# Scan of a state-space block: B put on the identity's diagonal and multiplied into du's transpose, in place of scaled copies of du

## The reference

```python
delta = softplus(dtp @ dt_w + dt_b)
A = -exp(A_log)
dA = exp(delta[..., None] * A)
dBu = (delta * xc)[..., None] * Bm[:, :, None, :]
def step(h, inp):
    dA_t, dBu_t, C_t = inp
    h = dA_t * h + dBu_t
    return (h, einsum('bds,bs->bd', h, C_t))
y = ys + xc * Dp
```

## Time and profile before

| | us |
|---|---|
| three runs | 457.71, 460.2, 460.31 |
| median | 460.2 |
| the profiled execution | 459.13 |
| its span, first to last instruction | 457.3 |
| PE / PEld busy | 404.7 / 265.1 |
| DVE / ACT / POOL busy | 284.4 / 234.2 / 138.6 |

### The profile page before, as it was taken

One profiled execution on the slowest core, in us unless ns is written; L12 is line 12 of the kernel. 1 busy time (PEld: TensorE's weight loads), 2 busy tenths in 40 slices (PEclk: granted clock), 3 DMA queues, 4 the chain that ended last, 5 costly groups with the idle time before them and its releaser, 6 DMA issues.

```text
span 457.3 us, 9931 instructions
## 1 busy us (share of the span) xinstructions
PE 404.7 (88%) x3990; PEld 265.1 (58%) x3990; DVE 284.4 (62%) x697; ACT 234.2 (51%) x433; POOL 138.6 (30%) x118
## 2 busy tenths in 40 slices
PE   3788998999989978997689999989999799999992
PEld 2445675546765836662466666754677456666662
DVE  5785985754757554326499888763466554444546
ACT  1225654737567055766699999314455552222220
POOL 5829643300013124130098989310001100000001
PEclk9899999999999988998899999999999999999997
DMA  7320000000000000003013332052000000000001
GB/s 184 78 72 1 3 4 2 1 3 1 4 4 0 1 0 2 1 0 93 16 69 97 112 97 76 1 187 90 3 3 4 2 0 1 0 0 2 0 1 46
DMA packets 17023, 14.42 MB, mean 32 GB/s; under 512 B 6435, under 2 KB 14147, under 8 KB 16979
## 3 DMA queue, kind: packets, MB, share of 16 engines
q1 hardware_dynamic: 15680, 13.09, 9.7%
q10 hardware_dynamic: 1299, 0.71, 0.5%
HBM read 13.22 MB, written 0.57 MB: 30 GB/s over the span
## 4 chain that ended last, share of the span: by engine, by line
PE 69%; DVE 13%; ACT 11%; issue 3%; DMA 1%; POOL 1%; ACTq 0%; POOLq 0%; DVEq 0%
PE PS L1695 7%; PE PS L1756 6%; PE PS L1760 6%; PE PS L1369 6%; PE PS L1787 6%; PE PS L1315 4%; PE PS L1301 4%; PE PS L1348 4%; ACT att L633 3%; PE PS L1682 3%; PE PS L1384 3%; PE PS L1611 2%; ACT att L795 2%; PE PS L1431 2%; PE PS L1310 2%
## 5 line engine op out<-in xcount | busy, mean ns | idle before, releaser
L633 ACT ACTIVATE att<-PS 77x512 f32<-77x512 f32 (+1 forms) x96 | 51.7, 591 | 45.7 <-PE PS L1372 45.7
L904 DVE TENSOR_REDUCE mxp<-PS 128x4 f32<-128x308 f32 (+1 forms) x96 | 48.0, 537 | 31.8 <-PE PS L1348 31.8
L496 POOL TENSOR_TENSOR rstd<-ve,neg_half 128x1 f32<-128x1 f32 x24 | 13.3, 556 | 120.1 <-DVE ve L966 120.1
L830 ACT ACTIVATE kM<-PS 128x512 f32<-128x512 f32 x32 | 19.1, 597 | 56.3 <-PE PS L1756 56.3
L1198 DVE TENSOR_TENSOR_SCAN big<-big,PS 128x768 f32<-128x768 f32 x22 | 38.2, 1746 | 7.2 <-PE PS L1682 7.2
L1254 DVE TENSOR_TENSOR big<-kM,PS 128x512 f32<-128x512 f32 x32 | 21.9, 688 | 27.3 <-PE PS L1760 26.0
L490 POOL TENSOR_TENSOR rstd<-ve,neg_half 128x4 f32<-128x4 f32 x6 | 6.2, 1032 | 103.7 <-DVE ve L860 103.7
L1301 PE MATMUL PS<-negsel,identb 128*128 128x512 bf16 x140 | 33.9, 386 | 2.2 <-DVE big L1006 1.7
L1756 PE MATMUL PS<-xT,V 128*128 128x512 f32 x64 | 32.9, 596 | 0.8 <-DVE xT L1242 0.8
L1760 PE MATMUL PS<-xT,V 128*128 128x512 f32 x64 | 32.7, 592 | 0.0
L1787 PEld LDWEIGHTS PS<-big 128*128 128x128 f32 x256 | 29.7, 192 | 3.3 <-issue 3.3
(11 more groups left out here) (349 smaller groups left out, 896.7 us busy)
## 6 DMA issues: line engine op xcount, KB each, us to landing
kM<-Cdram SPq DMA_DIRECT2D x6, 384.0 KB, 3.5
XH<-Cdram SPq DMA_DIRECT2D x5, 384.0 KB, 3.4
xT<-Cdram SPq DMA_DIRECT2D x5, 384.0 KB, 3.4
V<-in_L_ffn_Wg SPq DMA_DIRECT2D x1, 1024.0 KB, 5.4
V<-in_L_ffn_Wu SPq DMA_DIRECT2D x1, 1024.0 KB, 8.0
convw<-in_L_attn_conv_w SPq DMA_DIRECT2D x1, 512.0 KB
out_x<-X SPq DMA_DIRECT2D x2, 256.0 KB, 2.3
ctxN<-in_ctx ACTq DMA_DIRECT2D x1, 308.0 KB
```

The costliest lines, as they stand in the source:

```text
L633: A_(PT[0:nk, i % 2, g], bank4(at.bank("exp", i, g), nk), ACT.Exp, scale=at.scale)\
L904: V_.tensor_reduce(mxp[:, b % 3, g, 0:J], PS[:, at.bank("max", b, g), 0:J * nk].rearrange("p (j k) -> p j k", j=J), axis=AX.X, op=ALU.max) ...
```

## The change

`scale(s)` no longer scales duT. It multiplies the 128x128 identity by B for the tokens of piece k, which gives a diagonal matrix diagB, 128 x 128 for each of six pieces. `inputs(n)` multiplies: stationary operand duT (tokens x channels of half h), moving operand diagB; the result is du's piece with channels on partitions and each token's column scaled by its B. The call is a plain matmul instead of a transpose. The waits for duT go from `scale(0)`, and scale(0) and scale(1) stand ahead of decay(0). diagB has two sets of six in `att` and `qT`.

```diff
-    scaled = [[att[:, 1536 + 256 * k:1536 + 256 * (k + 1)] for k in range(NK)],
-              [qTflat[:, 256 * k:256 * (k + 1)] for k in range(4)] + [att[:, 3072 + 256 * k:3072 + 256 * (k + 1)] for k in range(2)]]
+    diagB = [att[:, 1536:1536 + W768].rearrange("p (k t) -> p k t", k=NK), qTflat[:, 0:W768].rearrange("p (k t) -> p k t", k=NK)]
...
         def scale(s):
             if s == 0:
                 dring.wait_copied(act, "BT")
-                act.wait_ge(event("duT0_copied"), 1)
-                act.wait_ge(event("duT1_copied"), 1)
             if s >= 2:
                 act.wait_ge(event("dBu_ready"), NH * (s - 1))
             for k in range(NK):
-                ins = A_(scaled[s % 2][k], duT[:, k, :], ACT.Identity, scale=BT[:, k, s:s + 1])
+                ins = A_(diagB[s % 2][:, k, :], ident[:], ACT.Identity, scale=BT[:, k, s:s + 1])
             ins.then_inc(event("scaled"), 1)

+        scale(0)
+        scale(1)
         decay(0)
         act.wait_ge(event("duT_ready"), 1)
         A_(duT[:, :, 0:128], PSflat[:, 4 * 512:4 * 512 + W768].rearrange("p (k d) -> p k d", k=NK), ACT.Identity)\
             .then_inc(event("duT0_copied"), 1)
         decay(1)
-        scale(0)
         decay(2)
-        scale(1)
...
             for k in range(NK):
-                ins = nc.tensor.transpose(dBu[n % NDB][:, 128 * k:128 * (k + 1)],
-                                          scaled[s % 2][k][:, 128 * h:128 * (h + 1)], ident[:])
+                ins = M_(dBu[n % NDB][:, 128 * k:128 * (k + 1)], duT[:, k, 128 * h:128 * (h + 1)], diagB[s % 2][:, k, :],
+                         start=True, stop=True)
             ins.then_inc(event("dBu_ready"), 1)
```

## The result

| | before | after |
|---|---|---|
| runs, us | 457.71 to 460.31 (6 runs) | 475.04 to 478.18 (6 runs) |
| median, us | 459.94 | 476.98 |
| profiled execution, us | 459.13 | 476.93 |
| its span, us | 457.3 | 475.1 |

The ratio is 1.0387, with a 95% interval of 1.0362 to 1.0412: 17.0 us slower by the medians, 17.8 by the ratio and by the two profiled executions. Forecast were 477.7 as a median (+17.5) and 476.6 for the profiled execution.

The account below looks back on a forecast made before the run. TensorE (PE) was taken to bound most of the scan, ScalarE its first quarter. Steps of 2.63 us gave +17.95, less 0.47 for the earlier start: +17.5 on 460.2, so 477.7 us, range 473.5 to 481.5.

Parts of the forecast that it names:

- The price of a call: TensorE's inputs: a float32 matmul is two records, 0.223 us against a transpose's 0.109; a step's inputs go from 0.66 to 1.34 us.
- rival 4: TensorE's inputs: a transpose is worth a factor of 4, 0.436 us a call; +57.4 us, 517.6; chance 1%.
- Rival 3: TensorE's inputs: weight loads of 0.19 us aren't hidden, 27 us on top, about 505; chance 2%.
- The start: Start of the scan: inputs(0) comes right after y_start, so the first scan and inputs(3) are 0.47 us earlier.
- The end of the stretch: From inputs(3) to the end of inputs(31), PE without a gap: 74.98 us instead of 57.03, ending near 305.7.
- ScalarE: Scaled copies of 128 instead of 256 elements: 1.70 us a step instead of 2.02, 10.3 us less busy, off the path.
- The bound of the kernel before: In the scan, ScalarE bounds the first quarter, PE the greater part from 247.5 us on, by the chain of waits.
- The bubbles: Gaps in PE's transpose groups during the scan, 1.77 us in all, put down to ScalarE's lateness; they go with the change.
- rival 2: TensorE's inputs: the added matmul costs what the transpose did, only the gains count; -2.9 us, 457.3; chance 4%.
- The moved calls: scale(0), scale(1) ahead of decay(0), no longer waiting for duT: decay(0) some 0.7 us later, duT's copy not moved.

Follow-up runs that it names:

- Experiment 1: Kernel before, scaled copies kept, but turned by a float32 matmul with the identity instead of a transpose: 478.97 us, ratio 1.0417.
- experiment 5: Changed kernel with duT and diagB in bf16, so a call is one record: 453.54 us, ratio 0.9889 to the kernel before.
- Experiment 3: Changed kernel with each diagonal written twice (256 columns), putting back ScalarE's old cost: 477.18 us, ratio 1.0372 to the kernel before.
- Experiment 4: Kernel before with scaled copies cut to 128 columns, second half's steps reading the first half's: 458.01 us, ratio 0.9971.
- experiment 6: Kernel before with h*C in bf16, the y accumulation two records in place of four: 457.48 us, ratio 0.9971.
- experiment 2: Changed kernel with scale(0) and scale(1) back behind decay(1) and decay(2): 476.54 us, ratio 1.0375 to the kernel before.
- experiment 8: Kernel before with diagonals and matmuls for s = 0 and 1 only, scaled copies and transposes after: 458.68 us, ratio 1.0004.
- 9: Changed kernel with duT, diagB and h*C all in bf16: 450.99 us, ratio 0.9841 to the kernel before.

## Why the prediction was right, and where it wasn't

- **The price of a call** (0.223 us from L1787's row, 1.34 a step): 1.34 in the chain at every step, 384 records. Experiment 1 shows that the kind of call alone does it, experiment 5 that the loss turns into a gain once the same call is one short record. The factor of 4 of rival 4 is refuted for this shape: 1.34 against 0.66 is 2.0. Rival 3 (weight loads that nothing hides) falls with the same 1.34.
- **The start**: inputs(0) was forecast for 225.63, the first scan for 227.18, inputs(3) for 230.72; the profile has 225.66, 227.19 and 230.74 (chain).
- **The end of the stretch**: forecast 230.72 + 74.98 = 305.70; the last accumulations begin at 305.79 (below, PE's records in order of time), 17.57 us after the 288.22 of the earlier trace rows.

```profile
304.45 1.50 PE L1679 MATMUL PS<-qT,big 128*128 128x128 f32 x12
305.79 2.75 PE L1692 MATMUL PS<-big,ident 128*128 128x512 f32 x8
```

- **ScalarE**: 128x128 copies of 386 ns (forecast near 385), 32% idle from 247 to 305 us (forecast 35% of the scan), 8.0 us less of busy time (forecast 10.3, a term that stood outside the sum); DVE's wait for PE up to 0.9 us a step, as forecast. Experiment 3 shows that the relief is worth nothing there.
- **The bound of the kernel before** was named too simply. The prediction read from the chain that PE was the bound from 247.5 us on, although it had ScalarE at 2.02 us a step and PE at 1.95. The chain's own starts settle it:

```profile
257.48 0.72 PE PS L1682 x6
...
285.64 0.79 PE PS L1682 x6
```

  That is 14 steps in 28.16 us, 2.01 a step: ScalarE's pace and not PE's. Experiment 4 relieved ScalarE and the step became 1.96; experiment 6 relieved PE and it stayed at 2.02. The chain hid this: PE's weight loads waited for ScalarE only 0.3 us at a time, and such a wait stands in the chain as a longer group of PE. For the sum nothing hung on it, since the change adds 0.68 us a step to PE, far more than the 0.07 us between the two.
- **The bubbles** had a cause that was only partly right. The prediction gave all 1.77 us to ScalarE's lateness. Experiment 4 shows that ScalarE's share goes when its copies are short, and that 0.34 us are the scan held up by VectorE's reduction. Both vanish at 2.63 us a step, so the sum wasn't touched; but rival 2 counted on all of the bubbles for its 2.9 us, and experiment 4, which has transposes and short copies, gave 1.3.
- **The moved calls**: the prediction had inputs(0) come right behind y_start, since the scaled operands no longer wait for duT; experiment 2 shows that the new place of the calls adds nothing to that.
- **The rest**: the forecast (+17.5) stands between the medians (+17.0) and the two profiled executions (+17.8), and both distances are inside the spread of the runs (2.6 us before, 3.1 after).

## What to carry to other kernels

In these traces a float32 transpose of 128x128 is one record (0.109 us from start to start) and a float32 matmul of the same shape two, each as long (0.112): before a transpose is replaced by a product that does more, count records, and look for a row of the same form elsewhere in the trace to price it. Halving the work of an engine is worth only what that engine contributes to the chain at the new pace; the same change lost 17 us or gained 5, by nothing but the room on TensorE. When two engines are both full, the chain can name one while the other sets the pace: divide a long stretch by its number of steps, compare that with each engine's own work, then relieve one engine at a time (here 1.3 us for ScalarE, 1.4 for TensorE: neither alone had much to give, both together 6).

## What the runs showed that I had not expected

- The low clock that follows TensorE's idle time ahead of the turning of du is not of one length. That idle time is 5.24 or 5.25 us in all eleven profiles, yet the six records of y_start behind it took 2.87 to 3.18 us in seven of them (2.97 in the changed kernel, 2.99 in the kernel before) and 4.32 to 4.45 in four (experiments 3, 6, 8 and 9). That is over 1 us in the time of a launch, as much as the smaller experiments were to measure. The changed kernel's and experiment 8's, from the timeline:

```profile
222.84 2.97 PE L1670 MATMUL PS<-kM,ident 128*128 128x512 f32 x6
...
220.86 4.45 PE L1678 MATMUL PS<-kM,ident 128*128 128x512 f32 x6
```

- The low clock also came inside the scan, in kernels whose TensorE has idle time there: in experiment 4 at 231 us, after 1.0 busy of 3 us; in experiment 5 just before 229, after 0.9 of 3; and in experiments 6 and 9, whose PE is busy for 17 of 28 us, for spells of their own. The kernel before had 1.4 busy of 3 us at the place that answers to experiment 4's, and no such spell in its profile. What decides between them is not shown.
